# A selective state-space layer with a mixture of experts: where dt's two parts are added

## The reference

```python
xn = layernorm(x)                       # x: (16, 1024, 256) f32
dt = softplus(xn @ dt_w.T + dt_b)       # (16, 1024, 256)
b, c = xn @ B_w.T + B_b, xn @ C_w.T + C_b        # 32 states
h = exp(A * dt_t) * h + (dt_t * x_t) * b_t       # for each t, per channel and state
y = sum over states of h * c_t + D_skip * x_t
moe: softmax(xn @ wg), top 2 of 8 experts, capacity 4096 rows each,
     relu(rows @ w1 + b1) @ w2 + b2, weighted by the gates
out = x + y + moe
```

## Time and profile before

| | us |
|---|---|
| median of three runs | 3822.43 (3817.44 to 3827.14) |
| profiled execution | 3817.81 |
| its span, first to last instruction | 3816.1 |
| VectorE busy | 3647.8 |
| GpSimd busy | 3261.9 |
| TensorE matmul busy | 3229.2 |
| ScalarE busy | 2564.6 |

### The profile page before, as it was taken

How to read it: one execution, slowest core, us unless ns; L and a number is a source line. 1 busy time by engine, 2 the same in 40 slices (tenths; PEclk the granted TensorE clock), 3 DMA queues, 4 the chain that set the end, 5 groups by cost and what they waited for, 6 DMA issues and landing times.

```text
span 3816.1 us, 64710 instructions
## 1 busy us (share of the span) xinstructions
PE 3229.2 (85%) x16548; PEld 2095.9 (55%) x16548; DVE 3647.8 (96%) x2281; ACT 2564.6 (67%) x4811; POOL 3261.9 (85%) x1722
## 2 busy tenths in 40 slices
PE   7776888888888888888888888888888888888887
PEld 4354555555555555555555555555555555555554
DVE  7787999999999999999999999999999999999998
ACT  3245677677776777767676767767676677767775
POOL 0017999999998999999998999999999999999996
PEclk9888999999999999999999999999999999999999
DMA  9975555555656556555656556465656555565555
GB/s 327 341 115 150 162 163 160 174 144 145 169 163 179 168 150 173 153 153 162 164 165 179 164 153 157 136 180 156 170 162 180 163 159 136 147 191 158 165 169 163
DMA packets 345305, 645.57 MB, mean 169 GB/s; under 512 B 49405, under 2 KB 221441, under 8 KB 344641
## 3 DMA queue, kind: packets, MB, share of 16 engines
q1 hardware_dynamic: 252018, 538.77, 43.8%
q0 software_dynamic: 67776, 85.24, 14.1%
q10 hardware_dynamic: 25104, 16.91, 2.0%
HBM read 515.55 MB, written 142.80 MB: 173 GB/s over the span
## 4 chain that ended last, share of the span: by engine, by line
issue 30%; DVE 25%; POOL 18%; PE 12%; ACT 7%; DMA 6%; DVEq 1%; POOLq 1%; SPq 1%; ACTq 0%
DVE hc L1214 12%; POOL u L1026 11%; DVE h L1225 10%; PE bank L639 3%; POOL out_rows L985 3%; PE bank L648 3%; ACT bank L798 2%; POOL xg L973 2%; DMA dt<-x 2%; DMA dt<-dt_rows 2%; PE bank L494 2%; ACT xgt L802 1%; POOL dtx_n L958 1%; ACT ht L840 1%; DMA bc_rows<-bcv 1%
## 5 line engine op out<-in xcount | busy, mean ns | idle before, releaser
L1026 POOL TENSOR_TENSOR u<-dtx,b_sb 128x1024 f32<-128x1024 f32 x1024 | 2514.5, 2523 | 146.1 <-DVE h L1225 102.7
L1225 DVE TENSOR_TENSOR_SCAN h<-bank,u 128x1024 f32<-128x1024 f32 x1024 | 2300.2, 2276 | 27.6 <-ACT bank L798 15.5
L798 ACT ACTIVATE bank<-dt,a_neg 128x1024 f32<-128x1024 f32 x1026 | 1129.0, 1108 | 401.7 <-DVE h L1225 309.7
L639 PE MATMUL bank<-xgt,w_sb 128*128 128x256 f32 x4096 | 1045.7, 400 | 257.3 <-ACT ht L840 216.6
L1214 DVE TENSOR_TENSOR hc<-h,bank 128x2048 f32<-128x2048 f32 x514 | 1163.6, 2264 | 44.9 <-ACT bank L868 44.3
L639 PEld LDWEIGHTS bank<-xgt,w_sb 128*128 128x128 f32 x4096 | 756.9, 195 | 636.7 <-issue 551.4
L648 PE MATMUL bank<-w_sb,ht 128*128 128x256 f32 x4096 | 936.4, 382 | 29.1 <-ACT o_sb L855 29.1
L648 PEld LDWEIGHTS bank<-w_sb,ht 128*128 128x128 f32 x4096 | 763.0, 191 | 221.4 <-issue 128.7
L840 ACT ACTIVATE ht<-bank,b_sb 128x256 f32<-128x256 f32 x1024 | 423.0, 463 | 288.4 <-PE bank L639 288.4
L598 PE MATMUL bank<-hc,rsum 128*32 128x512 f32 x4112 | 551.0, 608 | 2.5 <-DVE hc L1214 2.5
L985 POOL DMA_INDIRECT out_rows<-o_sb,sidx x258 | 415.4, 1610 | 55.6 <-issue 36.2
(11 more groups left out here) (114 smaller groups left out, 1821.9 us busy)
## 6 DMA issues: line engine op xcount, KB each, us to landing
b_sb<-bc_rows SPq DMA_DIRECT2D x258, 512.0 KB, 4.1
c_sb<-bc_rows SPq DMA_DIRECT2D x258, 512.0 KB, 4.2
dt<-dt_rows SPq DMA_DIRECT2D x132, 512.0 KB, 7.6
dtx<-dtx_rows SPq DMA_DIRECT2D x132, 512.0 KB, 5.2
w_sb<-w SPq DMA_DIRECT2D x18, 1024.0 KB, 7.7
dt_rows<-dt_n SPq DMA_DIRECT2D x137, 128.0 KB, 3.9
dtx_rows<-dtx_n SPq DMA_DIRECT2D x137, 128.0 KB, 1.8
out_rows<-y_sb POOLq DMA_DIRECT2D x34, 512.0 KB, 6.7
```

Of the source, the lines that this page charges most:

```text
L639: mm = pe.matmul(m_ps[:, c, :], w1_sb[:, kk, ch * P:(ch + 1) * P], xgt[:, kk, :], start=(kk == 0), stop=(kk == KD - 1))
L798: act.activation(a_ps[k % 2], dt[:, k % GPP, :], ACT.Exp, scale=a_neg[:, col:col + 1]).then_inc(a_ready, 1)
L1026: pool.tensor_tensor(u[:, k % UB, :], dtx[:, gp, :], b_sb[:, j, :], ALU.mult).then_inc(u_ready, 1)
L1225: dve.tensor_tensor_scan(h[:, k, :], a_ps[k % 2], u[:, k % UB, :], 0.0, ALU.mult, ALU.add).then_inc(scan_done, 1)
```

## The change

dt's two parts are added by TensorE, which multiplies each with the identity matrix and accumulates in bank 6, and ScalarE copies the sum to dt_n. ScalarE evacuates z twice, as relu into zv and as abs into za, and the abs of its own goes; the logarithm goes to za in SBUF right behind the exponential (k=4). TensorE adds inside moe_down(1), after two of its eight chunks, once weighing 3 has left the bank. ScalarE copies out at k=6, followed by the next step's first C copy, which is now ahead of decay 7 (it was behind it). Ahead of the loop VectorE still adds the ten first blocks, as a plain sum.

```diff
@@ tensor, moe_down(j)
                         for c in range(HC):
+                            if j == 1 and c == 2:
+                                sum_dt()
                             pe.matmul(m_ps[:, j, :], ht[:, c, j * P:(j + 1) * P], w2_sb[:, c, :],
+                    def sum_dt():
+                        pe.wait_ge(l_done, NG + 2 + st + 1)
+                        pe.wait_ge(hc_done, 4 * st + 5)
+                        settle(pe)
+                        pe.matmul(dt_ps, ident[:], zv[:].rearrange("p k t -> p (k t)"), start=True, stop=False)
+                        pe.matmul(dt_ps, ident[:], za[:].rearrange("p k t -> p (k t)"),
+                                  start=False, stop=True).then_inc(dt_summed, 1)
@@ scalar, evac_z
-                    ins = act.activation(zv[:, g, :], z_ps[:, g * Q:(g + 1) * Q], ACT.Identity, bias=dtb[:, g:g + 1])
+                    act.activation(zv[:, g, :], z_ps[:, g * Q:(g + 1) * Q], ACT.Relu, bias=dtb[:, g:g + 1])
+                    ins = act.activation(za[:, g, :], z_ps[:, g * Q:(g + 1) * Q], ACT.Abs, bias=dtb[:, g:g + 1])
@@ scalar, softplus and log_part
-                act.activation(za[:], zv[:], ACT.Abs).then_inc(za_done, 1)
-                act.wait_ge(za_done, p + 1)
                 act.activation(ze[:], za[:], ACT.Exp, scale=-1.0).then_inc(ze_done, 1)
-                act.activation(zl_ps, ze[:], ACT.Ln, bias=1.0).then_inc(l_done, 1)
+                act.activation(za[:], ze[:], ACT.Ln, bias=1.0).then_inc(l_done, 1)
+            def dt_out(p):
+                act.wait_ge(dt_summed, p - NG - 2 + 1)
+                act.wait_ge(dt_st, 16 * p + 1)
+                act.wait_ge(prep_done, p + 1)
+                settle(act)
+                act.activation(dt_n[:].rearrange("p k t -> p (k t)"), dt_ps, ACT.Copy).then_inc(dt_done, 1)
@@ scalar, the step
                             softplus(p)
+                            log_part(p)
                             c_copy(3)
...
                             down_out(0)
-                            act.wait_ge(hc_done, 4 * st + 5)
-                            log_part(p)
+                            dt_out(p)
+                            c_copy(0)
                         if k == 7:
-                            c_copy(0)
                             down_out(1)
@@ scalar, c_copy(0)
                             act.wait_ge(dt_done, p + 2)
+                            act.wait_ge(hc_done, 4 * st + 5)
@@ vector, prep_dt and the step
-                dve.scalar_tensor_tensor(out=dt_n[:], in0=zv[:], scalar=0.0, in1=zl_ps,
-                                         op0=ALU.max, op1=ALU.add).then_inc(dt_done, 1)
+                dve.tensor_tensor(dt_n[:], zv[:], za[:], ALU.add).then_inc(dt_done, 1)
...
-                prep_dt(NG + 2 + st)
```

More of the change, by code:

```diff
@@ L169, in ssm_moe @@
         bc_ps = bank[0:2 * N, 6, KD * Q:(KD + 1) * Q]
-        zl_ps = bank[:, 6, KD * Q:2 * KD * Q].rearrange("p (k t) -> p k t", k=KD)
+        dt_ps = bank[:, 6, 0:KD * Q]
         turn_ps = bank[:, 6, :].rearrange("p (k s) -> p k s", s=SL)
@@ L241, in ssm_moe @@
         v_done = sem("v_done")
-        za_done = sem("za_done")
         ze_done = sem("ze_done")
         l_done = sem("l_done")
+        dt_summed = sem("dt_summed")
         dt_done = sem("dt_done")
```

## The result

The changed kernel takes 3916.61 us (median of 6 runs, 3910.80 to 3921.01) against 3822.71 for the kernel before beside it: ratio 1.0244, 95% interval 1.0233 to 1.0255, 94 us slower. The forecast was 3882 in a range of 3835 to 3925. The direction and the mechanism of the steady steps held; one term, that of steps 0, had the wrong sign, and only the width of the range covers it.

The account below looks back on a forecast made before the run. VectorE, 96% busy, bounds the kernel now, with a TensorE-ScalarE ring 1.24 us behind that the change makes longer. Terms 11 + 12 + 27 + 23 + 10 - 17 = +66, less 2: +64 on 3817.81, so 3882 us, range 3835 to 3925.

Parts of the forecast that it names:

- steady steps: Steps 2, 3, 6 and 7 of a batch: 26.74 us for 26.57, +0.17 each, 64 of them, +11 us.
- steps 0: First step of each eight-step batch, at the loop's restart: +10 us over seven, -17 over eight with late loads.
- The ring: TensorE and ScalarE chain from weighing 2 via moe_down(1) and C's third copy to the next: 25.33 us, growing to 26.74.
- the pair: TensorE's two identity matmuls inside moe_down(1): nothing covers them, +0.90 us a step.
- the evacuation: ScalarE's activations of z, between prepare and the C copy, two becoming four: +0.51 us a step.
- the wait: TensorE's wait on the fourth weighing before the identity matmuls: no wait, by 0.4 us.
- steps 1 and 5: Second and sixth steps of a batch, 16 each: +1.41 and +1.68 us a step, +23 and +27 in all.
- step 4: Fifth step of a batch, which also turns y ahead of prepare: 27.31 us for 26.57, +0.74; 16, +12.
- VectorE's 40 us: VectorE's sum removed from the loop: 128 steps x 0.31 = 40 us of its own time, step 26.26 if nothing else holds.
- The copy out and the reordered C copy: ScalarE's copy of dt, then C's first copy of the next step: in ScalarE's idle time, cost 0.
- The rival of the low clock: TensorE's low clock stays in all eight late-load steps: +17 us more, 3899, up to 3910; chance 0.23.
- the third rival: The inserted wait stalls TensorE 0.3 to 0.35 us a step beyond the 0.90: +40, 3922 us; chance 0.13.

Follow-up runs that it names:

- the evacuation alone: Kernel before with z evacuated twice (relu and abs), VectorE still summing, no matmul, logarithm left in PSUM: 3838.11 us, ratio 1.0050.
- the matmuls alone: Kernel before with the two identity matmuls inserted, result unused, VectorE still summing, logarithm moved to SBUF: 3922.59 us, ratio 1.0286.
- the last experiment: Changed kernel with gates later, z evacuated once with abs and relu later, logarithm written into bank 6, one identity matmul; output wrong: 3820.43 us, ratio 0.9993.
- the filler: Changed kernel with four idle matmuls behind the last sum of states of each batch: 3936.97 us, ratio 1.0307.

## Why the prediction was right, and where not

**The ring: right, in all but one number.** 0.86 for the pair (forecast 0.90), 0.50 for the evacuation (0.51), no pause at the wait, steady steps 26.78 (26.74), steps 1 and 5 28.22 (28.25). The exception is step 4, 27.14 for 27.31: the turn of y ahead of prepare, read as 0.57 in the kernel before, lasts 0.44 in the changed one (2009.58 to 2010.01). It is shown, not argued: one matmul less and two more move the steady step by -0.43 and +0.86; the evacuation alone (26.58 to 26.63), and the matmuls alone (26.58 to 26.60), leave a steady step at VectorE's 26.57; and taking either the second evacuation or the gates off the ring brings it to 26.27 and 26.36. The trace puts 0.25 us on each further evacuation (2154.46, 2155.47: four in 1.01), below the 0.29 that the prediction estimated from the Trainium skill, "ScalarE: Activation LUTs", section "What ACT_TABLE_LOAD costs".

**VectorE's 40 us: right as the bound of another case.** They arrive only where the ring is shorter than 26.26, as in the last experiment.

**The copy out and the reordered C copy: right, 0.** VectorE doesn't wait ahead of weighing 0 in any steady step of the changed kernel.

**Steps 0: the step that failed.** The forecast said "the clock should mostly stay", -17 us over eight steps and +10 over seven. Measured: +10.5 over those eight and +22.5 over the seven, +33 in all. Two parts of the reasoning fell. First, that the rest of TensorE would shrink by the added 0.9 and the moved 0.5: the filler shows that work put ahead of the rest postpones it and doesn't fill it; the rests at even boundaries stay 2.7 to 3.8 (3.2 to 3.8 before). Second, that a rest of about 1.9 leaves the clock alone, which was read from one restart. The changed kernel lost it behind rests of 1.90 to 2.63, and the kernel before had lost it behind one of 1.45 and kept it behind 2.06: the length of this one rest doesn't decide. The trace of the kernel before also had the clock low behind three of its eight odd boundaries (rests 1.45, 1.68 and 2.28); the forecast counted two of these steps as undisturbed and the third with those that wait for dt's load. At the low clock moe_up(0) and often moe_up(1) take up to 3.75 instead of 1.97, on the ring.

The rival of the low clock, given 0.23, put it at 3899 to 3910; it happened, and at nearly all the boundaries, the odd ones too, so the time lies beyond even that. The nearest forecast in number is that of the third rival, 3922, a stall at the inserted wait. That is chance: it asked for steady steps of 27.1, and they are 26.78. Without steps 0 the forecast's terms make 3818 + 73 - 2 = 3889, and with the measured 33 for steps 0, 3922, 3 us above the profiled execution (3918.78).

**What times the rest.** The traces hold something that the prediction and the filler's reading left out. The profile lists a DMA queue of the kind "instruction", this row of the changed kernel's page (161 packets before, so one more for each of the fifteen restarts; 16 KB each):

```profile
q8 instruction: 176, 2.88, 0.3%
```

At the two restarts of the earlier trace rows one of its packets ends at 1844.39 and at 2060.11, and moe_up(0) begins at 1846.43 and 2062.01, 2.0 and 1.9 us later. In all 210 restarts of the fourteen traces this distance is 1.8 to 2.9 us, median 2.0, while the rests run from 0.65 to 6.26. So the rest is as long as this packet is late. That TensorE waits for it is inferred from these times; no run moved the packet alone. At even boundaries of the changed kernel it begins between 0.4 us before and 0.7 us after the end of TensorE's last instruction, and in the 2 us up to that end the 16 DMA engines are full (share 0.96 to 1.05, by the packets that start there); at odd ones it begins 1.3 to 2.1 us before, and the share is 0.07 to 0.35. With w2's load moved they are as full at even boundaries, 1.01 to 1.05, which fits that the move changed nothing: w2's load was issued only 0.8 us before the end of TensorE's last instruction (1217.74 and 1218.51).

**Still open:** which of the transfers ahead of an even boundary holds that packet up, and why a particular restart loses the clock. A version with the load of w1, which shares those boundaries, elsewhere wasn't tried. SyncE shares them too: its loop holds sixteen steps and restarts only there, and VectorE's holds one step (the description ahead gives all engines eight), and no run separates that from the loads. No version ran faster than the kernel before by more than its interval.

## What to carry to other kernels

Before an instruction is moved off the busiest engine, measure the ring that comes next: its start-to-start times, compared with the step, give the slack (here 1.24 us), and an edit that adds 1.4 to gain 0.3 is lost from the start (26.78 against 26.57). An engine at 96% sets the pace only where it doesn't wait. Then move things off the ring rather than off the engine: two evacuations less, or tiny gate activations placed one slot later, gave back 65 and 32 us here, while the same move in the kernel without that ring gave nothing.

## What the hardware showed that I had not expected

A VectorE sum of 128x256 takes 0.40 us with one operand in PSUM and up to 5.22 with both in SBUF beside GpSimd's products. The Trainium skill, page "SBUF — State Buffer", section "Who interferes with whom", says that a VectorE instruction with two inputs in SBUF contends with a GpSimd instruction that reads SBUF, over a pair of ports that is an exclusive lock, and that one with at most one SBUF input, outside its two-port modes, doesn't. The runs agree: 0.40 in all 138 sums with the logarithm in PSUM, and in SBUF a sum that started 0.27 us ahead of two products in a row (4.67 us) ended 0.28 behind them. It isn't every sum: one that began 0.17 us ahead of a product took 0.40 (1607.93). With the same evacuation, leaving the logarithm in PSUM, and so at its later place, was worth about 83 us (3921.5 against 3838.1).

A matmul that was to add onto what ScalarE had written in bank 6 overwrote it. The Trainium skill, page "PSUM — Partial Sum Buffer", section "The four PSUM rules", says that writes by ScalarE neither set nor clear the bit that makes a matmul add, so that earlier matmuls decide; the run agrees with its case of a clear bit.
